# Cross-attention keys, values, query weights and first rows made inside the last group of the self-attention

## What is computed

```python
x = x + _L0_attn_ref(_layernorm(x), w_fc, w_proj, ln_g, ln_b)       # self-attention block
    # y = layernorm(x) * g + b; q = y in 4 heads of 128
    # k = w_fc.reshape(-1, 128); v = w_proj.T.reshape(-1, 128)      (2048 fixed keys and values)
    # scores = q @ k.T; p = square(relu(scores)); out = p @ v; returns residual + out
x = x + _L0_xattn_ref(_layernorm(x), ctx, ctx, mask, Wq, Wk, Wv, Wo) # cross-attention, 16 heads of 64
    # q = x @ Wq; k = ctx @ Wk; v = ctx @ Wv  (ctx: 128 rows per sequence)
    # softmax(mask(q k^T / 8)) v, merged, @ Wo
x = x + _L0_ffn_ref(_layernorm(x), ...)                              # mixture of experts, not touched
```

## Time and profile before

| | us |
|---|---|
| median of 3 timed runs | 2922.22 |
| lowest, highest | 2921.61, 2923.0 |
| the profiled execution, whole | 2923.17 |
| its span (first to last instruction) | 2921.5 |
| TensorE busy in the span | 2803.1 |
| last scores of the self-attention done (start of the product behind them) | 763.08 |
| first scores of the cross-attention begin | 847.87 |

### The profile page before, as it was taken

The page is one execution under the profiler, slowest core; times in us unless marked ns, Lnnn a source line. Parts: engine busy times, 40 slices in busy tenths (PEclk is TensorE's granted clock), DMA queues, the critical chain, the costliest instruction groups (busy, mean ns, idle before and its releaser), DMA issues.

```text
span 2921.5 us, 46250 instructions
## 1 busy us (share of the span) xinstructions
PE 2803.1 (96%) x13288; PEld 2296.0 (79%) x13289; DVE 1788.9 (61%) x2741; ACT 1598.8 (55%) x2755; POOL 1065.4 (36%) x705
## 2 busy tenths in 40 slices
PE   7999999999769999999989999999999999999998
PEld 6888888888658888888867888887788888888886
DVE  6566665665466666666654444444876964776776
ACT  6888888887545555555531111111565743565665
POOL 5888888888611122212200000000233432332333
PEclk9999999999889999999999999999999999999999
DMA  1000000000221101111131112110987963876884
GB/s 62 26 26 11 25 25 29 25 11 11 90 83 44 36 32 51 40 44 43 39 114 58 58 67 70 64 57 29 320 316 258 336 248 123 288 279 224 289 285 179
DMA packets 185543, 322.71 MB, mean 110 GB/s; under 512 B 23656, under 2 KB 42088, under 8 KB 185472
## 3 DMA queue, kind: packets, MB, share of 16 engines
q1 hardware_dynamic: 173680, 295.56, 29.4%
q0 software_dynamic: 11792, 26.25, 2.7%
HBM read 286.86 MB, written 46.66 MB: 114 GB/s over the span
## 4 chain that ended last, share of the span: by engine, by line
PE 53%; issue 11%; DVE 3%; POOL 2%; ACT 2%; DMA 1%; ACTq 0%; DVEq 0%; POOLq 0%; SPq 0%
PE d_pG L1798 8%; PE d_pU L1798 8%; PE d_pD L49 3%; PE d_pD L47 3%; PE d_pD L48 3%; POOL b_S L727 2%; PE c_pD L47 2%; PE c_pD L49 2%; PE c_pD L48 2%; PE c_pG L47 2%; PE c_pG L49 2%; PE c_pG L48 2%; PE c_pU L47 2%; PE c_pU L49 2%; PE c_pU L48 2%
## 5 line engine op out<-in xcount | busy, mean ns | idle before, releaser
L156 POOL TENSOR_TENSOR a_pL<-a_p,a_pH 128x1024 fp32r<-128x1024 f32 x256 | 615.6, 2406 | 150.8 <-DVE a_p L344 149.2
L344 DVE TENSOR_TENSOR a_p<-a_r,a_pS 128x1024 f32<-128x1024 f32 x256 | 312.5, 1221 | 282.4 <-ACT a_r L163 276.1
L1054 DVE TENSOR_TENSOR e_wL<-e_raw,e_wH 128x1024 fp32r<-128x1024 f32 x384 | 450.4, 1218 | 34.8 <-PE d_pU L1798 26.2
L1049 ACT CAST e_wH<-e_raw 128x1024 fp32r<-128x1024 f32 x384 | 384.5, 1053 | 86.7 <-PE d_pD L49 59.2
L727 POOL TENSOR_TENSOR b_S<-b_S,b_ri 128x512 f32<-128x512 f32 x128 | 133.4, 1042 | 522.4 <-DVE b_ri L821 522.4
L163 ACT ACTIVATE a_r<-a_pS 128x1024 f32<-128x1024 f32 x256 | 262.3, 1024 | 100.1 <-PE a_pS L49 95.4
L163 ACT ACTIVATE a_pH<-a_r 128x1024 fp32r<-128x1024 f32 x256 | 272.0, 1062 | 9.0
L1290 POOL DMA_INDIRECT out<-d_og,c_iw x46 | 123.7, 2689 | 340.4 <-DVE d_og L1672 340.4
L47 PE MATMUL a_pS<-a_qH,a_kH 128*128 (+1 forms) x512 | 206.6, 403 | 0.6 <-DVE a_p L344 0.6
L47 PE MATMUL a_pO<-a_pH,a_vH 128*128 128x512 f32 x512 | 202.0, 395 | 0.6 <-POOL a_pL L156 0.6
L48 PE MATMUL a_pS<-a_qL,a_kH 128*128 (+1 forms) x512 | 202.5, 395 | 0.0
(11 more groups left out here) (304 smaller groups left out, 7272.4 us busy)
## 6 DMA issues: line engine op xcount, KB each, us to landing
e_raw<-in_L_ffn_routed_gate_w SPq DMA_DIRECT2D x256, 256.0 KB, 4.6
e_raw<-in_L_ffn_routed_up_w SPq DMA_DIRECT2D x256, 256.0 KB, 5.7
e_raw<-in_L_ffn_routed_down_w SPq DMA_DIRECT2D x128, 512.0 KB, 6.6
a_xb<-in_x SPq DMA_DIRECT2D x8, 1024.0 KB, 5.7
x<-a_o SPq DMA_DIRECT2D x32, 256.0 KB, 2.3
b_xb<-x SPq DMA_DIRECT2D x32, 256.0 KB, 2.7
b_xr<-x SPq DMA_DIRECT2D x32, 256.0 KB, 3.5
x<-b_xr SPq DMA_DIRECT2D x32, 256.0 KB, 3.0
```

The lines of the kernel that those rows point to most:

```text
L156: nc.gpsimd.tensor_tensor(pL[:, j % RING, :, :], p[:, j % 2, :, :], pH[:, j % RING, :, :].bitcast(F32), ALU.subtract).then_inc(s["low"], 1)
L344: v.tensor_tensor(p[:, j % 2, :, :], r[:, j % 2, :, :], pS[j % 2][:, :, :], ALU.mult).then_inc(s["p"], 1)
L1049: copy(self.wH[n][:, :, :], self.raw[n][:, :, :]).then_inc(self.s["high"], 1)
L1054: unit.tensor_tensor(self.wL[n][:, :, :], self.raw[n][:, :, :], self.wH[n][:, :, :].bitcast(self.F32), self.sub).then_inc(self.s["low"], 1)
```

## The change

`self_attention` no longer has a block and tiles of its own. It gives back functions for each engine (`sync`, `gpsimd`, `scalar`, `vector`, `tensor`), and those of `cross_attention` call them, handing in hooks: `late(j)` is called in every step j of group 7, `begin` after it. All tiles of both parts are placed by one plan of addresses (`Place`). What the setup did now stands in the hooks:

- SP issues Wk as four pieces of 512 KB (256 columns, all rows: runs of 1 KB) as soon as group 7's rows are transposed; each piece of Wv follows when the keys of its slot are split (`kL`), Wq after the values (`v_ps`), Wo after the last product. The second sequence's keys are stored by SP.
- ACT splits the 12 pieces in steps 1 to 28 (`W_HIGH_AT`), DVE one step later; Wo is split in steps 2 to 6 of the first group of the cross-attention.
- PE transposes ctx in steps 6 and 8, makes the keys in steps 9, 11, 13, 15 (4 turns of 24 products of 256 columns) and the values in steps 17, 19, 21, 23 (4 turns of 12 products of 512 columns), and transposes the first two tiles of rows in step 28, the other two in `begin`. All of it up to the values goes through one buffer, a_pX; a turn waits until DVE has split the one before.
- DVE makes the row scales of tiles 0 to 23 in steps 0 to 6 and of tiles 24 to 31 in the first group of the cross-attention; the first rows are normalized in steps 24, 25, 29, 30.
- POOL zeroes kH, kL and vH at the start of the program and vL in steps 8 to 11.
- `add_out` adds into a_base in place, and the stores read a_base.

The diff, cut to its core:

```diff
-        block = ctx.enter_context(nc.Block())
-        @block.sync
-        def _(sp):
+    def sync(sp, late):
...
+            if last:
+                late(store)
+                return
...
-            add_out(GROUPS * NH - 1, GROUPS - 1, NH - 1, False)
-            out_stats(GROUPS * NH - 1, GROUPS - 1, NH - 1)
+        ending(lambda: add_out(k, g, h), lambda: out_stats(k, g, h))
...
+    K_AT, V_AT = (9, 11, 13, 15), (17, 19, 21, 23)
+    W_HIGH_AT = {1: (0, 0), 4: (0, 1), 7: (0, 2), 10: (0, 3), 13: (1, 0), 15: (1, 1), 17: (1, 2), 19: (1, 3),
+                 22: (2, 0), 24: (2, 1), 26: (2, 2), 28: (2, 3)}
+    NORM_AT = (24, 25, 29, 30)
+    X_AT = 28
...
+        # sync, late
+            sp.wait_ge(a["xt"], HEADS)
+            for n in range(PIECES):
+                load_weights(0, n)
+            sp.wait_ge(a["score"], PRODUCTS - NH * ANP)
+            sp.dma_start(cx[:, :, :], ctx_in.rearrange("b k c -> k b c")).then_inc(s["c_in"], 16)
+            store(g - 1, NH - 1)
+            for n in range(PIECES):
+                keep_keys(n)
+                load_weights(1, n)
+                if n == 1:
+                    store(g, 0)
...
+        # scalar
+        def late(j):
+            if j == 7:
+                c_high(0)
+            if j == 8:
+                c_high(1)
+            for n in range(PIECES):
+                if j == K_AT[n] + 1:
+                    if n == 0:
+                        act.wait_ge(s["zero"], 3)
+                    k_high(n)
+            for n in range(2 * NB):
+                if j == V_AT[n] + 1:
+                    v_high(n)
+            if j in W_HIGH_AT:
+                w_high(*W_HIGH_AT[j])
...
+        # vector
+        def late(j):
+            if j < 7:
+                if j == 0:
+                    dve.wait_ge(a["seen"], HEADS - NH - 1)
+                row_scales(j, 0, KNOWN - GT)
+            if j == 8:
+                c_low(0)
+            if j == 9:
+                c_low(1)
+            for n in range(PIECES):
+                if j == K_AT[n] + 2:
+                    k_low(n)
+            for n in range(2 * NB):
+                if j == V_AT[n] + 2:
+                    v_low(n)
+            if j - 1 in W_HIGH_AT:
+                w_low(*W_HIGH_AT[j - 1])
+            for i in range(GT):
+                if j == NORM_AT[i]:
+                    norm(0, i)
...
+        # vector, first group of the cross-attention
+                if first and 3 <= j < 3 + PIECES:
+                    wo_low(j - 3)
+                if first and j == 1:
+                    dve.wait_ge(a["seen"], HEADS)
+                if first and 1 <= j:
+                    row_scales(j - 1, KNOWN - GT, TILES)
...
+        # tensor
+        def keys(n):
+            pe.wait_ge(s["w_low"], n + 1)
+            pe.wait_ge(s["cL"], 2)
+            wait(pe, s["kL"], n)
+            for j in range(2):
+                for c in range(KC):
+                    at = (slice(None), n, c, slice(j * P, (j + 1) * P))
+                    m = split_matmuls(nc, pK[:, j, :, :], (wH[at], wL[at]), (cH[:, c, :, :], cL[:, c, :, :]), c == 0, c == KC - 1)
+            m.then_inc(s["k_ps"], 1)
...
+        def begin(products, out_transpose):
+            products(ANP - 3)
+            pe.wait_ge(a["p"], PRODUCTS - 1)
+            x_transpose(2, 2, 0)
+            x_transpose(3, 3, 0)
+            products(ANP - 2)
+            products(ANP - 1)
+            pe.wait_ge(s["xL"], GT)
+            pe.wait_ge(s["w_low"], 3 * PIECES)
+            pe.wait_ge(a["p"], PRODUCTS)
+            query(0, 0)
+            out_transpose()
+        attention["tensor"](pe, late, begin)
```

More of the change, by code:

```diff
@@ new lines, in self_attention, with heads_at @@
+    counts = ("ident wf_in wp_in gb_in x_in stat own kvt kvH kvL normed based"
+              " xt qt qH qL score relu p pH low pv oT ot added seen out0 out1").split()
+    s = {n: sem(n) for n in counts}
+    LINKS = 29
+    STATS_AT, SCALES_AT, NORM_AT = 4, 10, 15
+    BASE_AT = {21: 0, 22: 1, 24: 2, 25: 3}
+    HEADS_AT = {19: 0, 22: 1, 25: 2, 28: 3}
+    FIRST_HEADS_AT = {1: 1, 4: 2, 7: 3}
+    def heads_at(j, first, last):
+        out = [(0, FIRST_HEADS_AT[j])] if first and j in FIRST_HEADS_AT else []
+        return out + ([(1, HEADS_AT[j])] if not last and j in HEADS_AT else [])
@@ new lines, in body @@
+                for dg, q in heads_at(j, first, last):
+                    x_transpose(g + dg, q)
+                if last:
+                    late(j)
+        groups(pe, body)
+        ending(lambda c: products(GROUPS * NH - 1, NH - 1, c, False), lambda: out_transpose(GROUPS * NH - 1))
+    return {"sync": sync, "gpsimd": gpsimd, "scalar": scalar, "vector": vector, "tensor": tensor, "s": s,
+            "steps": STEPS * GROUPS, "heads": NH * GROUPS, "NH": NH, "STEPS": STEPS, "NPAIR": NPAIR, "pX": pX}
@@ L699, in outputs @@
                 free(g, i)
-        for i in range(GT):
-            wait(sp, s["normed"], i - 1)
-            load(i, i)
         def body(g, b, pb, first, last):
@@ L760, in body, with begin @@
+        def begin(out_copy):
+            act.wait_ge(a["score"], PRODUCTS)
+            for i in range(GT):
+                x_high(i, i)
+            out_copy()
+            act.wait_ge(a["p"], PRODUCTS)
+            act.wait_ge(a["pH"], PRODUCTS)
+            q_high(0, 0)
+        attention["scalar"](act, late, begin)
         def body(g, b, pb, first, last):
@@ L767, in body @@
                         x_high(GT * g + GT + i, i)
+                if j == 2 and first:
+                    act.wait_ge(a["seen"], HEADS)
+                    for i in range(2):
+                        act.wait_ge(a[f"out{i}"], 16 * HEADS // 2)
                 if j > 1 or not first:
@@ L775, in body @@
                     q_high(n + 1, 0)
+                if first and 2 <= j < 2 + PIECES:
+                    wo_high(j - 2)
         groups(act, body)
@@ L858, in body, with begin @@
+        def begin(add_out, out_stats):
+            for i in range(GT):
+                x_low(i, i)
+            q_low(0, 0)
+            add_out()
+            out_stats()
+            dve.wait_ge(s["m_in"], 16)
+            dve.wait_ge(a["pv"], PRODUCTS)
+            dve.wait_ge(a["low"], PRODUCTS)
+        attention["vector"](dve, late, begin)
         def body(g, b, pb, first, last):
@@ new lines, in late @@
+        def late(j):
+            if j == 6:
+                c_transpose(0)
+            if j == 8:
+                c_transpose(1)
+            for n in range(PIECES):
+                if j == K_AT[n]:
+                    keys(n)
+            for n in range(2 * NB):
+                if j == V_AT[n]:
+                    new_values(n)
+            if j == X_AT:
+                pe.wait_ge(s["vL"], 2 * NB)
+                x_transpose(0, 0, 0)
+                x_transpose(1, 1, 0)
+        def begin(products, out_transpose):
[10 more added lines that the diff above has]
+            out_transpose()
```

978 lines of the change are left out of this document (500 added, 478 removed).

## The result

The changed kernel takes **2911.9 us** (median of 6 runs, 2911.34 to 2914.23) against 2922.26 for the kernel before on the same chip: a ratio of 0.9967, with a 95% interval from 0.9956 to 0.9977. It gains 10.4 us where 20 were forecast. The profiled execution's span went from 2921.5 to 2910.3 us.

The account below looks back on a forecast made before the run. PE bounds both sides of the boundary, itself a chain of transfers and splits: 2923.17 - 73.8 + 24.6 + 22.8 + 6.5 = 2903.3, as a median 2902 us; range 2884 to 2914.

Parts of the forecast that it names:

- -73.8: Boundary from the last self-attention scores to the first cross-attention scores: shrinks from 84.79 to 11.0 us, removing 73.8.
- 24.6: Group 7 on PE: moved keys, values and transposes count in full, as PE has no free time; adds 24.6 us.
- Adding in place, the stores and POOL's zeroing: In-place sum, stores and zeroing before group 0: put at nothing, within 1 us either way.
- in slices 12 and 13: Where the profile page before the change shows PE's visible hole and the dip of its granted clock.
- The waits of the turns, 21.9: Group 7: PE waits nine times for DVE's previous low part, 21.9 us; 22.8 with 0.1 for each restart.
- Row scales ... within DVE's free time: Scales of tiles 0 to 23 in group 7: 0.6 to 1.5 us per step, hidden in DVE's free time.
- DVE's pieces at 1.14: Weight splits in steps 1 to 29 of group 7: 1.14 us each on DVE, hidden by its 1.56 free per step.
- so it is no wait: After group 7's last scores: POOL's last part frees the last product at 4.98 us, before PE's 5.2, costing nothing.
- The change does it warm: Work added to PE in group 7 runs at full clock, 24.6 us; at half clock it would be double.
- the measured step with its pause decides for me: First cross-attention step, at clock 1.00 despite a 1.5 us pause, taken as evidence that group 7's clock holds.
- The clock rival: Group 7: PE's repeated 2 to 3 us pauses halve its clock, +45 us, 2947 us in all; chance 8%.
- The first cross group, 6.5: First cross-attention group: DVE gets 9.0 us of new work with hardly any slack; 6.5 us let through.

Follow-up runs that it names:

- Experiment 1: Kernel before the change, only its tile addresses altered: small tiles set last, 2910.4 us against 2923.4; the changed kernel's whole address plan, 2910.6 us.
- Experiment 3: Changed kernel with GpSimd's subtraction for the low part of p cut to 16 of 512 columns in group 7 (results wrong): 2900.7 us.
- the fastest kernel: Changed kernel with turns set later, row scales in PSUM, weights' low parts moved earlier, Wo's low parts on GpSimd, last scales moved: 2869.1 us.

## Why the prediction went wrong

**The sum was right in its sign and wrong in its reasons.** Two errors of opposite sign met: 22.6 us of the forecast gain did not come, and 12 to 13 us came from something that I had not weighed. That the time is within 10 us of the forecast of 2902 is luck. Against the kernel whose tiles stand alike, the rest of the change was forecast at -26.4 us in A (-73.8 + 24.6 + 22.8) and +6.5 in B, and brought -5.3 and +8.0. Of A, group 7 up to its last scores is 64.6 us longer where 24.6 + 22.8 = 47.4 were forecast, and from there to the first scores of the cross-attention it takes 14.4 us where 11.0 were.

- *"Adding in place, the stores and POOL's zeroing ... I put at nothing":* **a term is missing here.** The address plan was not weighed at all, and it made the measured gain. Experiment 1 gives it 12 to 13 us, all of 10.4. I read the plan for overlaps of tiles and not for where they begin.
- *The hole "in slices 12 and 13":* it is in slices 11 and 12; nothing in the sum hangs on it.
- *The waits of the turns, 21.9:* 23.0. The working held in seven of nine turns, within 0.4 us. The turn of step 15 waited 4.24 instead of 2.3, behind a low part of weights that GpSimd had held (2.84 us), and that of step 8 waited 1.25 instead of 2.45; that these two nearly cancel is luck too.
- *"Row scales ... within DVE's free time" and DVE's pieces at 1.14:* **this step failed.** DVE had free time, but GpSimd took it. The earlier trace rows showed GpSimd at work 2.41 of every 2.78 us, and the weights' split of the earlier trace rows was measured beside nothing of GpSimd's but a memset, which has no input (b_vL, 3.51 us from 781.53 on) and did not hold it: 3.50 us for three pieces. I did not put these together. Its price in A, waits of PE: a_p 6.0, b_xn 1.64, a_pL 1.55: 9.2 us, where the prediction had "so it is no wait" for the last a_pL. Experiment 3 gives 12.1 back with GpSimd's work gone: these 9.2, 0.5 of the turns and 2.4 of PE's busy time.
- *"The change does it warm", "the measured step with its pause decides for me":* **this step failed too.** A pause of 1.5 us in the earlier trace rows said nothing of pauses of 3 to 4, and in the earlier trace rows the one of 7.36 us had spoken. PE is busy for 134.37 us in A; in the fastest kernel the same 613 matmuls take 123.52:

```profile
666.21:793.78 127.57, 123.52 (x613) 103.43 (x612) 85.33 (x147) 89.17 (x107) 91.85 (x37) 1.00 0.29 87
```

  The difference is 10.9 us; by my estimate the five low stretches make 8.8 of it (5 x 3.5 / 2), the rest I can't place (slower first products behind each wait may be part of it). The clock rival (8%) had its mechanism right and its price of 45 us four times too high, because the clock came back each time after about 3.5 us. The rule of the Trainium skill that I had set against the trace ("TensorE: Matmul & The Clock Gate", "Why this matters for your kernels": no idle gaps between bursts) was the better guide.
- Together: 9.2 + 10.9 + 0.2 (turns: 23.0 against 22.8, restarts included) = 20.3 of the 21.1 us that A is short of its forecast. With B's 1.5 less and the addresses' 12 to 13 more, 20 forecast come to 10, as measured.
- *The first cross group, 6.5:* 8.0. PE's waits there rose by 8.0 - 2.1 = 5.9, so that term was nearly right; the other 2.1 are PE's busy time (55.93 instead of 53.82 us), with one more low stretch of the clock, behind a wait of 1.95 us at 888.

## What to carry to other kernels

When a change touches the address plan, compare where each tile that TensorE reads begins modulo 512 bytes: here small tiles between large ones cost 13 us of 2922, and it can be had without any other change. Before work is given to DVE's free time, see whether GpSimd is at work then; if so, give it a PSUM input, or set it directly behind the instruction that GpSimd waits for. And where PE takes turns on one bank, count the chain of the other engines from the scores to the low part, and set the turn that far behind: waits of 2 to 4 us cost themselves and often the clock behind them.

## What the runs showed of the hardware that I had not expected

- Matmuls of 512 fp32 columns follow each other at 0.227 us when the rows and weights that alternate begin alike modulo 512 bytes, and at 0.230 to 0.233 on average when pH and pL stand 448 bytes off (92.50 us a group against 90.97, and 92.25 at 64 bytes off); 512 bytes off is free (90.94), and so is the other place that was tried for all tiles (90.95).
- GpSimd's subtraction (2.40 us, two SBUF inputs) holds DVE instructions of 0.24 us for 2.39 and 2.40; with one PSUM input the same instructions take 0.19 beside it. The other way round, DVE's 1.22 us make GpSimd's 2.40 into 3.31.
- In the changed kernel PE's clock fell to its lower level for about 3.5 us behind six single waits of 1.95 to 4.24 us, in work that was otherwise dense, and not behind three others (2.01, 2.54 and 2.66); in its second trace one low stretch lasted 6.9 us, and in two other kernels one stood behind a wait of 1.64. A change that takes 15.2 us of such waits away gained 21.8.
